# A fused graph-transformer layer: 80 products with an unused result, given to TensorE in three stretches of the expert routing

## What is computed

```python
logits = jnp.einsum('bsd,de->bse', x, gate_w) + gate_b
probs = jax.nn.softmax(logits, axis=-1)
top_probs, top_idx = jax.lax.top_k(probs, 2)
top_probs = top_probs / jnp.sum(top_probs, axis=-1, keepdims=True)
...
hidden = jax.nn.silu(h1) * h2
expert_out = jnp.einsum('bseh,eho->bseo', hidden, w3)
return jnp.einsum('bseo,bse->bso', expert_out, dispatch)
```

## Time and profile before

| | us |
|---|---|
| median of 3 executions | 1144.78 |
| lowest and highest of them | 1144.42 and 1147.15 |
| the profiled execution's own time | 1145.69 |
| its span, from first to last instruction | 1143.9 |
| TensorE busy in the span | 1046.2 (91%) |

### The profile page before, as it was taken

One profiled execution on the slowest core, in us unless ns is written; L12 is line 12 of the kernel. 1 busy time (PEld: TensorE's weight loads), 2 busy tenths in 40 slices (PEclk: granted clock), 3 DMA queues, 4 the chain that ended last, 5 costly groups with the idle time before them and its releaser, 6 DMA issues.

```text
span 1143.9 us, 23536 instructions
## 1 busy us (share of the span) xinstructions
PE 1046.2 (91%) x7924; PEld 987.0 (86%) x7924; DVE 895.5 (78%) x1334; ACT 670.5 (59%) x1023; POOL 757.6 (66%) x717
## 2 busy tenths in 40 slices
PE   4897999999999999999999989973599999999992
PEld 2465899999999999999999989962499999999992
DVE  7877888888999888888888826768677777777760
ACT  2562766666666666666666535430176766776760
POOL 5447777777777777777777555401456777777742
PEclk9998999999999999999999999975899999999996
DMA  8211444444444444444444302223178888888854
GB/s 237 75 52 51 144 143 143 142 140 140 142 141 144 146 144 140 142 139 143 139 143 146 92 3 91 67 83 105 50 207 229 236 226 221 240 234 232 231 122 130
DMA packets 115687, 165.13 MB, mean 144 GB/s; under 512 B 15393, under 2 KB 88150, under 8 KB 115542
## 3 DMA queue, kind: packets, MB, share of 16 engines
q1 hardware_dynamic: 83942, 95.11, 26.1%
q0 software_dynamic: 31104, 68.19, 24.0%
q10 hardware_dynamic: 560, 0.79, 0.3%
HBM read 145.55 MB, written 21.68 MB: 146 GB/s over the span
## 4 chain that ended last, share of the span: by engine, by line
PE 85%; DVE 8%; issue 3%; ACT 1%; DMA 1%; DVEq 0%; POOL 0%; POOLq 0%; ACTq 0%; SPq 0%
PE ps L1443 24%; PE ps L1619 16%; PE ps L1454 15%; PE ps L1631 8%; PE ps L1397 8%; PE ps L1498 3%; PE ps L1371 2%; PE ps L1508 2%; PE ps L1521 2%; PE ps L1606 1%; PE ps L1535 1%; PE ps L1364 1%; DVE st L919 1%; PE ps L1380 1%; DVE xnT L1288 1%
## 5 line engine op out<-in xcount | busy, mean ns | idle before, releaser
L1443 PE MATMUL ps<-fr 128*128 128x256 f32 x2352 | 307.0, 287 | 3.4 <-DVE fr L981 3.4
L1443 PEld LDWEIGHTS ps<-fr 128*128 128x128 f32 x2352 | 289.5, 192 | 4.3 <-DVE fr L981 4.2
L566 POOL DMA_INDIRECT big<-xn_rows,srcs x200 | 218.4, 1092 | 60.8 <-issue 60.8
L566 POOL DMA_INDIRECT hgx<-xn_rows,srcs x192 | 209.9, 1093 | 58.5 <-issue 58.5
L718 ACT ACTIVATE h1f<-ps,b 128x512 f32<-128x512 f32 x196 | 124.1, 684 | 166.9 <-PE ps L1397 165.7
L1454 PEld LDWEIGHTS ps<-oh,big 128*128 128x128 f32 x1568 | 191.1, 193 | 8.6 <-DVE big L1117 0.5
L1619 PE MATMUL ps<-fr 128*128 128x256 f32 x1536 | 192.0, 285 | 2.7 <-issue 1.4
L1619 PEld LDWEIGHTS ps<-fr 128*128 128x128 f32 x1536 | 188.5, 194 | 3.3 <-issue 1.8
L1454 PE MATMUL ps<-oh,big 128*128 128x96 f32 x1568 | 189.6, 274 | 0.4 <-DVE big L1126 0.4
L981 DVE TENSOR_TENSOR fr<-h1f,fr 128x1024 fp32r<-128x1024 f32 x98 | 120.1, 1225 | 52.1 <-ACT fr L721 52.0
L1307 DVE TENSOR_TENSOR fr<-big,fr 128x1024 fp32r<-128x1024 f32 x96 | 117.4, 1223 | 30.3 <-ACT fr L833 30.0
(11 more groups left out here) (189 smaller groups left out, 1374.7 us busy)
## 6 DMA issues: line engine op xcount, KB each, us to landing
big<-in_w SPq DMA_DIRECT2D x128, 256.0 KB, 3.8
rbf<-in_rbf SPq DMA_DIRECT2D x98, 256.0 KB, 3.0
big<-in_w SPq DMA_DIRECT2D x32, 512.0 KB, 4.0
xn_rows<-xn SPq DMA_DIRECT2D x38, 128.0 KB, 1.7
big<-xn_rows,srcs POOLq DMA_INDIRECT x200, 3.1
out<-out_rows SPq DMA_DIRECT2D x1, 3125.0 KB, 12.0
hgx<-xn_rows,srcs POOLq DMA_INDIRECT x192, 3.2
out_rows<-x_nodes SPq DMA_DIRECT2D x3, 768.0 KB, 3.7
```

The source lines that it names most:

```text
L566: pool.indirect_dma_start(hg[i % HB][:, s, :], None, xn_d[:, :], bass.IndirectOffsetOnAxis(srcs[:, col:col + 1], 0))\
L1443: last = mm(ps[:, 2 + 4 * p + s // 2, (s % 2) * D:(s % 2 + 1) * D], h1s[p][a][:, c, s * P:(s + 1) * P], W2s[b][:, c, :], start=c == 0 and ...
```

## The change

The change defines `keep_clock(n)`, which issues `n` products of a 128 by 128 piece of `U1s` with 512 columns of `UMs`. They go to bank 5 of PSUM, each one over the last, and nobody reads them. They signal no semaphore. `keep_clock(12)` stands behind the last gate logits and ahead of the wait for `s_m12`, after a wait for `s_x1` (the last node sums have left bank 5). `keep_clock(44)` stands between the counting products and the first `place`, `keep_clock(24)` between the last `place` and the first `turn`.

```diff
             gate_logits(NT - 1, 0)
+            def keep_clock(n):
+
+                for _ in range(n):
+                    mm(ps[:, 5, :], U1s[0][:, 0, 0:P], UMs[0][:, 0:DC, :].rearrange("p k d -> p (k d)"),
+                       start=True, stop=True)
+            pe.wait_ge(s_x1, NB + 2)
+            keep_clock(12)
             pe.wait_ge(s_m12, 1)
             mf = m12.rearrange("p t e -> p (t e)")
             mm(ps[:, 0, 0:TX], before[:, :], mf, start=True, stop=True)
             mm(ps[:, 1, 0:TX], ones[:, :], mf, start=True, stop=True).then_inc(s_cnt, 1)
             pe.sem_inc(s_tab, 2)
+            keep_clock(44)
             def place(c, p, start=False, stop=False):
...
             pe.sem_inc(s_xsp, 2)
             pe.sem_inc(s_h, 8)
             pe.sem_inc(s_o, 2)
+            keep_clock(24)
             pe.wait_ge(s_tabi, 1)
```

## The result

| us | before | changed |
|---|---|---|
| median of 20 executions each | 1145.7 | 1143.4 |
| lowest and highest | 1142.82, 1147.32 | 1139.07, 1145.16 |
| the profiled execution's own time | 1145.69 | 1143.69 |
| its span | 1143.9 | 1141.9 |

The ratio is 0.9976, with a 95% interval of 0.9967 to 0.9985: 2.7 us faster, between 1.7 and 3.8. The interval leaves out "no change", and the gain is under 0.3% of the time. Five of the changed kernel's executions lie at 1139.1 to 1141.7, fifteen at 1142.8 to 1145.2.

A forecast was written before the change was run, and what follows sets the result against it. TensorE was taken to bound the kernel nearly everywhere. Gains of 0.8 (counting products), 0.2 (table) and 0.3 (transposes and first up step), together 1.3 us, off 1144.78 gave 1143.5 us, range 1140.6 to 1145.9.

The forecast's parts named there:

- The case that I called the likeliest: Routing: the full clock is partly held; 1143.5 us, own range 1142.0 to 1144.8, chance 0.60.
- Cost of the products: Waits in the routing: they cover all 80 products, 0.23 us each at full clock, 0.46 at low; no path cost.
- Counting products, 0.8 of 1.5: Two counting products behind the gate logits: full clock worth up to 1.5 us, 0.8 taken as gain.
- some nine of the twelve run low: Stretch ahead of the counting products: about nine products at low clock (4.1 us), three at full (0.7), ending at 772.7.
- Table, 0.2 of 1.0: First two table steps: full clock worth up to 1.0 us, 0.2 taken as gain.
- The two gains hardly come together: Counting products and table: winning the first leaves a 3.8 us pause ahead of the table, so both gains hardly coincide.
- Transposes and first up step, 0.3 of 2.3: First transposes and first `expert_up`: full clock worth up to 2.3 us, 0.3 taken, the 24 products mostly falling back.
- The three pauses as a rule: Idle TensorE in one trace: pauses of 2.70 and 2.29 us lost the clock, 1.75 kept it; used to judge remaining pauses.
- the third rival: From the experiments: the clock's moments differ so much between executions that pause length alone decides nothing; no chance given.
- The rival of a clock held throughout: Routing: the three stretches bridge every wait, full gain of 4.8 us, 1140.0; chance 0.16 including nearly so.
- Outlasting the wait: Ahead of the table: the 44 all at low clock take 20.2 us, table 6.2 us late, 1151.0; chance 0.06.

The follow-up runs named there:

- over80: The changed kernel with 80 products for the 44 ahead of the table; ratio to the kernel before 1.003 (0.9989 to 1.0072).
- first12: The changed kernel with only the twelve products ahead of the counting products kept; ratio to the kernel before 0.9989 (0.9944 to 1.0034).
- filled: The changed kernel with 16, 58 and 35 products for 12, 44 and 24, plus five behind the first transposes; three runs, ratios 0.9854, 0.9944, 0.9937.
- changed_again: The changed kernel run again without an edit; ratio to the kernel before 0.9917 (0.9867 to 0.9968).
- second44: The changed kernel with only the 44 products ahead of the table kept; too few comparable runs for a ratio; count to table 17.07 us, table 21.29.
- unchanged: The kernel before, run without an edit as if it were a changed one; ratio 1.0007 (0.9958 to 1.0056).
- wider: filled with added products also in pauses of the node update and ahead of the last down step; ratio to the kernel before 0.9924.
- wider28: wider with 28 products for 16 ahead of the counting products; two runs, ratios to the kernel before 0.9968 and 0.9947.

## Why the prediction came out as it did

The forecast was 1143.5 us and the time is 1143.4. That the two agree so closely is luck: the median of the kernel before moved from 1144.78 (3 executions) to 1145.7 (20), and the gain is 2.3 us between medians, 2.7 by the ratio, for the 1.3 that I forecast. The case that I called the likeliest came true: the clock is held in part, the time lies in the range, and the change is too small for 0.3% to tell. The gain was forecast at about half of what it is.

*Cost of the products.* Right. 0.231 us each at the full clock (over80), 0.46 at the low one (5.47 us for twelve), and all three stretches lie in their waits.

*Counting products, 0.8 of 1.5.* Mis-sized. The full clock gave 1.4 in the changed kernel's first profile, in first12, and in all three of filled; 0.75 in changed_again. The step behind it, "some nine of the twelve run low", failed: in the first profile all twelve ran low, they took 5.5 us instead of 4.8, and the pause was 1.48 us instead of 2.0. The clock rose only behind them, 6.0 us after their start and 1.0 ahead of the count. In the six other profiles in which the same stretch begins low the rise came 4.4 to 5.9 us after its start, and I had taken 3.9 to 4.3 from two rises. The trace of the kernel before had a longer stretch of low clock that I did not weigh: from 757.16 us on, behind a pause of 2.72 us, it does its last transposes and gate logits at the low clock, nearly without a pause, and has not risen when they end at 767.92.

```profile
757.16 1.12 PE L1364 MATMUL ps<-ident,xn 128*128 128x128 f32 x4 [2.72 <-DVE xn L930]
764.00:765.00 1.00, 1.00 (x6) 0.98 (x5) 0.48 (x2) 0.37 (x1) 0.00 (x0) 0.50 0.03 11
```

*Table, 0.2 of 1.0.* Mis-sized: 0.4 in the first profile, 0.97 in changed_again against the profile before. I had let the long pause take the clock from the table. A pause of 4.04 us took it only 0.5 us into the work, and for 3.4 us; the pauses of 3.04 us (changed_again) and 2.80 (second44) ahead of the table didn't take it at all. "The two gains hardly come together" was wrong: both profiles of the changed kernel have both in part.

*Transposes and first up step, 0.3 of 2.3.* About right: 0.0 in the first profile. In changed_again the transposes took 0.63 us, but the up step 5.26 to the next transposes: 7.34 us together, 0.5 under unchanged and 0.1 over the first profile of the kernel before. The transposes gain by the clock where they meet it, 0.63 us for 1.09 in nine profiles. The Trainium skill (TensorE: Matmul & The Clock Gate, the part on transposes) says that the full clock does not engage for them; the measurements decide against that here.

*The three pauses as a rule.* The weakest step, as I had said. The pause of 2.29 us ahead of the last down step, the same in eleven profiles in which nothing fills it, cost the clock in five (4.4 to 4.6 us for the step) and not in six (3.1). In unchanged it did not:

```profile
1205.72 3.11 PE L1631 MATMUL ps<-fr 128*128 128x256 f32 x24 [2.29 <-issue]
```

Ahead of the counting products pauses of 1.48, 1.72 and 1.81 us kept it (changed, over80, first12), and one of 1.92 lost it by the second of them (changed_again). Ahead of the table 2.80 and 3.04 us kept it. So in these profiles a longer pause is not always worse than a shorter one, and one trace's pauses don't say what a pause does: the third rival holds for the pauses of 1.9 to 4 us. For short ones it does not: in the three profiles of filled, whose pauses in the routing are all under 0.9 us, the clock is full from the count to the second transposes.

*The rival of a clock held throughout* was priced at 4.8 us. filled, which does hold it, gets 4.6 by the timelines. *Outlasting the wait* was priced at 0.23 us a product beyond the cover; over80 paid that at the table (4.0 us) and won 1.4 of it back behind.

What stays open: what makes the five executions at 1139.1 to 1141.7. No profile of one was taken. The first profile (1143.69 us) had the last down step at 4.6 us and the transposes slow; with the step at 3.1, as in changed_again, it would have been at 1142.2. So part of the spread can be the last down step, which the change doesn't touch, and whether the up step also met the full clock in these five is not shown: in both profiles of the changed kernel it met the low one. Open too is what decides when the clock falls in a pause of 2 to 4 us.

## What to carry to other kernels

Where the bounding engine waits and comes back at half its clock, count what it does at the low clock on the chain: that sum (here 4 to 5 us) is all that filler in these waits can bring. Here it came in full only in the versions that left no pause over 0.9 us, up to the work itself and across it; the versions with pauses of 1.5 to 4 us got part of it. Size filler by its cover at the clock at which it will start, because a stretch sized for a low start is too short when an earlier one has raised the clock (wider against wider28). Filler that outlasts its wait delays the work behind it (over80, 4.0 us at the table). Judge such a change on several profiles: one execution of one kernel differs from the next by 1.5 us in a single step.

## What was not expected of the hardware

The clock rose while TensorE was idle, 0.5 us behind the last of twelve products (773.2 us), and in the first profile it outlived a pause of 4 us, to fall with the work already running again.

The same kernel, unchanged, took 1145.7 us (median) in the runs of the result and 1234.5 to 1248.5 beside the experiments, on four chips. In the profile of unchanged all of the difference, 85.5 us, lies ahead of the last part of the node update. VectorE waits there on the biases (line 1103) and the one-hot operands (line 1109) of the edge loop for something that the profile puts down to "remote", which the first profile doesn't have at all. These waits come to 85.2 us, though other waits got shorter. What they wait for was not looked for, and whether the chips themselves make the difference isn't shown. From VectorE's waits in unchanged (who waited for whom, us in total, times, longest):

```profile
DVE big L1103 <- remote: 54.9, 13, 9.1
DVE oh L1109 <- remote: 30.3, 24, 3.4
```
